# Expert stage: the down projection issued one slot tile at a time between the next expert's gate and up groups, its results signalled, copied out and scattered in two parts

## The reference, cut to what matters

```
x = x + attention(layernorm(x))
xf = layernorm(x)
buf[e, slot] = xf[token]                      # dispatch, 640 slots per expert
h     = silu(buf @ wg) * (buf @ wu)           # per expert, 128 -> 256
out_e = h @ wd                                # per expert, 256 -> 128
x = x + shared(xf) + sum_k gate_k * out_e[expert_k, slot_k]
```

## Time and profile before

| | us |
|---|---|
| median of 3 runs | 897.61 |
| lowest and highest | 888.08, 899.48 |
| profiled execution, its span | 904.6 |

### The profile page before, as it was taken

One profiled execution on the slowest core, in us unless ns is written; L12 is line 12 of the kernel. 1 busy time (PEld: TensorE's weight loads), 2 busy tenths in 40 slices (PEclk: granted clock), 3 DMA queues, 4 the chain that ended last, 5 costly groups with the idle time before them and its releaser, 6 DMA issues.

```text
span 904.6 us, 24570 instructions
## 1 busy us (share of the span) xinstructions
PE 724.0 (80%) x7521; PEld 563.5 (62%) x7521; DVE 534.0 (59%) x2192; ACT 360.9 (40%) x853; POOL 415.1 (46%) x548
## 2 busy tenths in 40 slices
PE   3798888988978788898888858888888888877960
PEld 1565656665646565575665637777777777777540
DVE  3476756556577676656666656545454454543598
ACT  4465544454455445444454423332323232322200
POOL 4125343353343434334344350555555555556555
PEclk9698776676798878767788859999999999998985
DMA  8991000000000000000000002423233333421355
GB/s 268 358 390 35 14 20 15 12 23 12 12 22 10 20 9 15 10 7 14 6 7 6 6 8 84 125 76 105 76 114 107 114 115 103 126 75 32 122 182 167
DMA packets 52338, 68.37 MB, mean 76 GB/s; under 512 B 9505, under 2 KB 31807, under 8 KB 52304
## 3 DMA queue, kind: packets, MB, share of 16 engines
q1 hardware_dynamic: 38240, 53.56, 18.4%
q0 software_dynamic: 9216, 11.97, 4.4%
q10 hardware_dynamic: 4848, 2.40, 0.9%
HBM read 34.89 MB, written 39.99 MB: 83 GB/s over the span
## 4 chain that ended last, share of the span: by engine, by line
PE 52%; another core or an unknown queue 19%; issue 10%; DVE 10%; ACT 6%; POOL 1%; ACTq 1%; DVEq 1%; POOLq 0%
PE bank L693 9%; PE bank L864 7%; PE bank L680 6%; PE bank L674 5%; PE bank L663 5%; PE bank L657 3%; PE bank L701 3%; DVE x_all L1246 3%; DVE mx L1044 2%; PE bank L733 2%; ACT hact L607 2%; PE bank L817 2%; PE bank L756 1%; PE bank L747 1%
## 5 line engine op out<-in xcount | busy, mean ns | idle before, releaser
L463 POOL DMA_INDIRECT pair_results<-yout,yidx x160 | 157.2, 982 | 143.4 <-ACT yout L625 104.0
L447 POOL DMA_INDIRECT expert_slots<-xfe,sidx x128 | 127.0, 992 | 141.5 <-DVE sidx L1148 108.3
L864 PE MATMUL bank<-xgT_parts,wgu_parts 128*128 128x320 f32 x768 | 147.2, 344 | 46.4 <-ACT hact L607 46.4
L864 PEld LDWEIGHTS bank<-xgT_parts,wgu_parts 128*128 128x128 f32 x768 | 125.9, 208 | 57.3 <-ACT hact L607 50.3
L519 ACT ACTIVATE pt<-bank 128x512 f32<-128x512 f32 x128 | 76.2, 596 | 182.2 <-PE bank L680 164.9
L1259 DVE TENSOR_TENSOR hact<-hact,bank 128x320 f32<-128x320 f32 x128 | 57.1, 481 | 140.2 <-ACT hact L607 133.1
L1044 DVE TENSOR_REDUCE mx<-bank 128x4 f32<-128x512 f32 x128 | 87.3, 683 | 32.5 <-PE bank L663 19.7
L421 POOL TENSOR_TENSOR pout<-pin,mhalf 128x3 f32<-128x3 f32 (+2 forms) x36 | 29.9, 830 | 127.4 <-DVE pin L970 127.4
L890 PE MATMUL bank<-wdn,hact 128*128 128x128 f32 x640 | 82.7, 288 | 2.3 <-issue 2.3
L890 PEld LDWEIGHTS bank<-wdn,hact 128*128 128x128 f32 x640 | 82.5, 207 | 2.5 <-issue 2.5
L623 ACT COPY yout<-bank 128x512 f32<-128x512 f32 x32 | 18.7, 585 | 162.2 <-remote 151.0
(11 more groups left out here) (148 smaller groups left out, 1335.1 us busy)
## 6 DMA issues: line engine op xcount, KB each, us to landing
expert_slots<-fill SPq DMA_DIRECT2D x32, 322.5 KB, 6.5
xg<-expert_slots SPq DMA_DIRECT2D x32, 322.5 KB
pair_results<-rload SPq DMA_DIRECT2D x32, 256.0 KB
rload<-pair_results SPq DMA_DIRECT2D x16, 512.0 KB, 4.0
wgu<-in_L_ffn_wg_dram SPq DMA_DIRECT2D x32, 128.0 KB
wgu<-in_L_ffn_wu_dram SPq DMA_DIRECT2D x32, 128.0 KB
wdn<-in_L_ffn_wd_dram SPq DMA_DIRECT2D x32, 128.0 KB
pair_results<-yout,yidx POOLq DMA_INDIRECT x160
```

The source lines that it names most:

```text
L447: g.indirect_dma_start(out=slots_d, out_offset=bass.IndirectOffsetOnAxis(ap=sidx[:, tr.b, k:k + 1], axis=0), in_=xfe[:, tr.b, k, :], in_of ...
L463: g.indirect_dma_start(out=pairs_d, out_offset=bass.IndirectOffsetOnAxis(ap=yidx[:, c, j:j + 1], axis=0), in_=yout[:, c, j, :], in_offset= ...
L864: last = mm(bank[2 + 2 * w + h][:, 0:CH], wgu_parts[:, e.b, wp, w, h * P:(h + 1) * P], xgT_parts[:, e.b, xp, ch * CH:(ch + 1) * CH], start ...
```

## The change

It takes effect in the expert stage alone.

- PE: after `gate_up(0)` comes slot tile 0 of the down projection, then a group of `gate_up(1)`, then tile 1, a group, tile 2, a group, tile 3, a group, tile 4. `down_done` is raised twice for each expert: after tile 3 (bank 6 is complete) and after tile 4.
- ACT: the silus of chunk 1 stand ahead of the two copies out. Each copy has its own wait: the first for `down_done >= 2*ed + 1`, the second for `2*ed + 2`.
- POOL: the first four scatters wait for the first copy, the fifth for the second; each part has its own `hold`, a nop that carries the wait.
- Every other wait on `down_done` counts double (ACT ahead of chunk 0, SP ahead of the down weights).

```diff
@@ SP
-                sp.wait_ge(S.down_done, e - 1)
+                sp.wait_ge(S.down_done, 2 * (e - 1))
@@ POOL
-                    pool.wait_ge(S.y_evac, 2 * e + 2)
-                    hold(pool)
                     for j in range(ST):
+                        if j == 0 or j == 4:
+                            pool.wait_ge(S.y_evac, 2 * e + (j // 4 + 1))
+                            hold(pool)
                         g.indirect_dma_start(
@@ ACT
-                    wait(act, S.down_done, e.n - 1)
+                    wait(act, S.down_done, 2 * (e.n - 1))
                     silu(0)
+                def silu_last(h):
+                    act.wait_ge(S.gu_done, 8 * e.n + (4 + 2 * h + 1))
+                    a.activation(hact[:, e.b, h, CH:2 * CH], bank[2 + h][:, 0:CH], ACT.Silu).then_inc(S.h_act, 1)
+                if e is not None:
+                    silu_last(0)
+                    silu_last(1)
                 if ed is not None:
-                    act.wait_ge(S.down_done, ed.n + 1)
+                    act.wait_ge(S.down_done, 2 * ed.n + 1)
                     wait(act, y_sent[ed.b], 16 * ST * ed.half)
                     a.copy(yout[:, ed.b, 0:4], bank[6][:, :].rearrange("p (j d) -> p j d", d=D))\
                      .then_inc(S.y_evac, 1)
+                if ed is not None:
+                    act.wait_ge(S.down_done, 2 * ed.n + 2)
                     a.copy(yout[:, ed.b, 4:ST], bank[7][:, 0:D].rearrange("p (j d) -> p j d", d=D))\
                      .then_inc(S.y_evac, 1)
-                if e is not None:
-                    silu(1)
@@ PE
+                def down(j):
                     for h in range(2):
+                        last = mm(bank[6 + j // 4][:, j % 4 * D:(j % 4 + 1) * D],
+                                  hact[:, ed.b, h, j * P:(j + 1) * P], wdn[:, ed.b, h, :],
+                                  start=(h == 0), stop=(h == 1))
+                    if j == 3 or j == ST - 1:
+                        last.then_inc(S.down_done, 1)
...
-                    gate_up(0)
+                    for h in range(2):
+                        for w in range(2):
+                            gate_up(0, h, w)
                 if ed is not None:
                     pe.wait_ge(wdn_arrived[ed.b], 16 * (ed.half + 1))
                     pe.wait_ge(S.h_mul, 4 * ed.n + 4)
                     wait(pe, S.y_evac, 2 * ed.n)
-                    for j in range(ST):
-                        for h in range(2):
...
-                    last.then_inc(S.down_done, 1)
-                if e is not None:
-                    gate_up(1)
+                    down(0)
+                for j in range(1, ST):
+                    if e is not None:
+                        gate_up(1, (j - 1) // 2, (j - 1) % 2)
+                    if ed is not None:
+                        down(j)
```

More of the change, by code:

```diff
@@ L855, in expert_step, with gate_up @@
             def expert_step(en, e, ed):
-                def gate_up(ch):
-                    for h in range(2):
-                        for w in range(2):
-                            wait(pe, (S.h_act, S.h_mul)[w],
-                                 4 * e.n + (2 * ch + h - 1) if not isinstance(e.n, int) or e.n else 2 * ch + h - 1)
-                            for wp, xp in ((0, 0), (0, 1), (1, 0)):
-                                last = mm(bank[2 + 2 * w + h][:, 0:CH],
-                                          wgu_parts[:, e.b, wp, w, h * P:(h + 1) * P],
-                                          xgT_parts[:, e.b, xp, ch * CH:(ch + 1) * CH],
-                                          start=(wp + xp == 0), stop=(wp == 1))
-                            last.then_inc(S.gu_done, 1)
+                def gate_up(ch, h, w):
+                    wait(pe, (S.h_act, S.h_mul)[w],
+                         4 * e.n + (2 * ch + h - 1) if not isinstance(e.n, int) or e.n else 2 * ch + h - 1)
+                    for wp, xp in ((0, 0), (0, 1), (1, 0)):
+                        last = mm(bank[2 + 2 * w + h][:, 0:CH],
+                                  wgu_parts[:, e.b, wp, w, h * P:(h + 1) * P],
+                                  xgT_parts[:, e.b, xp, ch * CH:(ch + 1) * CH],
+                                  start=(wp + xp == 0), stop=(wp == 1))
+                    last.then_inc(S.gu_done, 1)
+                def down(j):
+                    for h in range(2):
+                        last = mm(bank[6 + j // 4][:, j % 4 * D:(j % 4 + 1) * D],
[3 more added lines that the diff above has]
+                        last.then_inc(S.down_done, 1)
                 if en is not None:
@@ L887, in expert_step @@
                     wait(pe, S.y_evac, 2 * ed.n)
-                    for j in range(ST):
-                        for h in range(2):
-                            last = mm(bank[6 + j // 4][:, j % 4 * D:(j % 4 + 1) * D],
-                                      hact[:, ed.b, h, j * P:(j + 1) * P], wdn[:, ed.b, h, :],
-                                      start=(h == 0), stop=(h == 1))
-                    last.then_inc(S.down_done, 1)
-                if e is not None:
-                    gate_up(1)
+                    down(0)
[4 more added lines that the diff above has]
+                        down(j)
             lagged_steps(pe, expert_step, NE, True)
```

## The result

| | us |
|---|---|
| after, median of 4 runs | 928.22 (923.32 to 929.30) |
| before, median of the 4 runs beside them | 894.68 (888.08 to 899.48) |
| ratio, 95% interval | 1.039, 1.030 to 1.047 |
| span of the profiled executions, after and before | 926.0, 904.6 |

The forecast was 903 with a range of 845 to 914: the kernel got slower by 3.9%, outside the range and on the side that had the smallest chance. The two profiled executions differ by 21.4 us, less than the medians do (33.5), since that of before lay some 10 us above its median.

What follows compares the result with a forecast made beforehand. The expert stage was taken as bound by PE's marks held until POOL's scatter burst lands, beat 8.90 us. +0.15 per step over 29 steps, +4.4, and +0.8 at the first burst gave +5.2: median 903, range 845 to 914.

Steps and rivals of the forecast that it cites:

- The ring: Expert stage's beat: marks released, copies 0.75, way to first scatter 0.84, burst 6.09, landing about 1.25; 8.93 against 8.90 us measured.
- the gone hold: Expert stage if PE's marks are no longer held: beat falls to PE's 6.7 or POOL's 6.4, say 6.8 us; 837.
- Both `down_done` marks lie behind the held 3.48: held, and released together: PE's marks after slot tiles 3 and 4, due 3.6 and 4.5 us into POOL's burst, both come at its landing.
- the boundary: Time in POOL's scatter burst after which PE's marks are held: between 1.75 and 3.48 us.
- the sum: Expert stage, each step: +0.32 for the second silu, -0.17 for copy B, +0.15 us; over 29 steps +4.4.
- copy B leaves the ring: POOL starts scattering on copy A alone, so copying counts 0.585 instead of 0.75 us per step, -0.17.
- The other side: Second `down_done` misses the release, four scatters land alone, ring 11.1 us; 967 in all steps; chance 0.11 shared with POOL drained.
- Its lighter case: Second `down_done` misses the release in a third of the expert steps: +22 on 903, 925 us.
- The third rival: Hold needs an unbroken run of small fp32 matmuls, or the array is late and groups help; 837 or 877; chance 0.18.
- The silus: Chunk 1's silus on ACT: first passes early, nothing on the beat; second held ahead of copy A, +0.32 us per step.
- SP's queue and POOL's second hold: SP's down-weight load released at the same landing as before, POOL's extra wait free; nothing taken, +0.5 kept for the range.
- its cover: PE's idle stretch of 2.1 us until the landing, into which its first groups run up to 0.75 us sooner.

Runs made afterwards that it cites:

- x_four: The kernel before with each expert's fifth scatter left out; 870.07 us, ratio 0.956.
- x_direct: The kernel before with five plain transfers to scratch memory in place of each expert's five scatters; 833.16 us, ratio 0.915.
- plain10_4: The kernel before with ten plain transfers to scratch memory in place of each expert's five scatters, compared where marks are held; 841.88 us, ratio 0.926.
- p_joint: The changed kernel with POOL waiting for both copies before an expert's first scatter; ratio 0.989 (900.64 us) where marks are held, 1.035 (752.25 us) where not.
- p_gap: The changed kernel with POOL also waiting, after an expert's fifth scatter, until all five have landed; 902.22 us, ratio 0.989.
- p_split: The kernel before with two marks, two-part copy and two-part scatter, but its own PE and ACT order; ratio 0.993 where marks are held, 0.996 twice where not.
- a_again: The changed kernel unaltered, compared again with the kernel before where no mark is held; ratio 1.014.
- p_best: The changed kernel with joint start, POOL's wait for landing, slot tiles earlier on PE and last silu behind the copies; 810.56 us, ratio 1.115, marks not held.

## Why the prediction was wrong

- **The ring, right.** Marks, copies, burst and landing made 8.93 of 8.90; the burst less a scatter took 1.38 off a step (1.48 over the flow) for 1.28 (x_four), and without indirect transfers the beat fell to 6.3 and 6.5 (x_direct, plain10_4), where I had put the gone hold at 6.8.
- **The wrong step: "Both `down_done` marks lie behind the held 3.48: held, and released together".** The first one passed in mid-burst, in p_joint for 25 of 31 experts, in p_gap for 30, in after for 11; the second came 1.0 to 1.2 us behind the burst's last scatter in most steps of p_joint, and 1.0 to 3.8 behind it in after, where the next burst had begun meanwhile. I had taken the boundary from marks behind another order of PE and treated it as a time. p_split shows that the time is not what decides.
- **The consequence that no case had: POOL.** I had written what the release needs, the landing of the burst's last transfer, and what the change takes away, the wait for both copies, without joining them: that wait was what kept POOL from beginning again until the marks were out. In the sum the early start of POOL stood as a gain (copy B leaves the ring, -0.17). In the trace of after POOL came 1.9 us early (mean of 11 experts) and the ten experts behind paid 3.3 us each; the stage, for which the sum had 29 x 0.15 = +4.4, took 14.8 longer.
- **The other side was the nearest rival in form and wrong in mechanism.** It had the two marks come apart, but with the first at the release and the second missing it, and four scatters landing alone. What happened is that the first came early and the fifth scatter always found its copy in time. Its lighter case gave 925, near the 928 measured, and that is chance.
- **The third rival had the condition right and the consequence wrong.** It said that the hold to the end needs an unbroken run of small matmuls and that groups between them help; p_split against p_joint shows just that. But I priced it as a hold that is gone, at 837 to 877, and the marks that escaped made the kernel slower through POOL.
- **The silus.** The first did pass before the ring needed it. The second, put at +0.32 on the ring, came out in mid-burst too (617.79, ahead of copy A) and cost nothing: p_joint's beat is 8.40, not 9.05.
- **SP's queue and POOL's second hold, put at nothing:** nothing in the traces speaks against it.
- **What would show it wrong** was named rightly: copies A and B more than half a us apart (619.21 and 621.34), and copy A inside the burst of the expert before.
- **The interleaving of PE was costed at nothing, with the landing's idle time as its cover.** Where marks are held, as in the trace I forecast from, that was so (p_joint 0.989). Where marks are not held the cover is gone and the order alone costs 3.5 to 4.8%.

## What to carry to other kernels

When a change loosens a wait, ask what else that wait held back: here POOL's wait for both copies was also the pause in which PE's held marks came out, and starting 1.9 us earlier cost 3.3 us one expert later. A boundary read from the trace as a time (marks pass before so many us) holds only for the order of work it was read from; put the moved work's own neighbours beside it before using it. And read which resource a stage waits for in the comparison at hand, since the same program was bound by held marks in some and by PE and POOL in others, and p_joint's edit changed sign between them (0.989 and 1.035).

## What the runs showed of the hardware that I had not expected

- PE's marks are held while POOL issues indirect transfers, and not while it issues plain ones of the same length: beat 8.90 against 6.50 (plain10_4, from the second copy to the thirtieth), in comparisons where before takes 895 to 914 us.
- The hold is not all or nothing: with PE's work interleaved marks came out inside the burst, 1.8 us (617.37 to 619.21) and 1.9 us (672.46 to 674.40) late, and behind an unbroken run of small matmuls 3.65 us (656.35 to 660.00) late.
- In other comparisons nothing is held, the same program takes 725 us, and the mean granted clock of an execution is 0.92 to 0.96 where it was 0.80 to 0.85.
- The landing of a scatter behind a burst is not a fixed time: median 1.32 us after its end on POOL in a_again, 1.33 in p_gap, 2.2 (up to 2.98) in p_best.
